# Reordering the partitions of a recurrent stage, summing the step size in PSUM, and moving one C product to GpSimd

## The reference, cut to what matters

```python
h = layer_norm(x)                              # x: 8 sequences x 256 x 128
u, z = split(h @ in_w)                         # 256 channels each
u = silu(conv(u))                              # 4 taps
dbl = u @ xw                                   # 64 + 16 + 16 columns: rank, B, C
dt = softplus(dbl[:64] @ dtw + dtb)            # step size, 256 channels
h_t = exp(dt_t * A) * h_(t-1) + (dt_t * u_t) * B_t     # 16 states for each channel
y_t = sum over states of h_t * C_t,  + u * D
x = x + (y * silu(z)) @ ow
```

## Time and profile before

| | |
|---|---|
| median of three runs | 1708.91 us (1708.18 to 1709.97) |
| the profiled execution | 1705.7 us |
| its span, first to last instruction | 1704.0 us |
| recurrent stage in it | scans from 499.97 to about 1315.9 us |
| busy in the whole span | PE 1337.6, DVE 1387.7, ACT 1311.6, POOL 1075.3 us |
| mean granted TensorE clock | 0.924 of 2.4 GHz |

### The profile page before, as it was taken

The page is one execution under the profiler, slowest core; times in us unless marked ns, Lnnn a source line. Parts: engine busy times, 40 slices in busy tenths (PEclk is TensorE's granted clock), DMA queues, the critical chain, the costliest instruction groups (busy, mean ns, idle before and its releaser), DMA issues. The chain is left out here.

```text
span 1704.0 us, 25209 instructions
## 1 busy us (share of the span) xinstructions
PE 1337.6 (78%) x7544; PEld 694.5 (41%) x7547; DVE 1387.7 (81%) x2394; ACT 1311.6 (77%) x2978; POOL 1075.3 (63%) x714
## 2 busy tenths in 40 slices
PE   6777898996677776867776877767756899899989
PEld 4554555553322222332222332222322466566543
DVE  4655788896529999999999999999998588778835
ACT  4444787884658999999999999999975788777730
POOL 2001566661048999999999999999996254444410
PEclk9999899997978889999989988999977999999979
DMA  3000000001045434455434545443440511121000
GB/s 105 2 1 2 1 2 2 1 2 26 7 174 208 178 122 173 164 210 199 165 132 165 200 167 199 174 146 147 185 150 25 185 51 51 51 99 50 1 1 25
DMA packets 70229, 168.19 MB, mean 99 GB/s; under 512 B 20420, under 2 KB 40152, under 8 KB 56664
## 3 DMA queue, kind: packets, MB, share of 16 engines
q1 hardware_dynamic: 68680, 166.17, 27.1%
q10 hardware_dynamic: 1168, 0.53, 0.1%
q0 software_dynamic: 256, 0.01, 0.0%
HBM read 131.04 MB, written 35.65 MB: 98 GB/s over the span
## 5 line engine op out<-in xcount | busy, mean ns | idle before, releaser
L1785 POOL TENSOR_TENSOR ma_hs<-ma_dtuR,ma_Bt 128x1024 f32<-128x1024 f32 x192 | 449.4, 2369 | 12.3 <-DMA ma_dtuR<-ma_dtu_d 6.9
L914 POOL TENSOR_TENSOR x_pr<-x_pr,x_rec 128x512 f32<-128x512 f32 x256 | 267.9, 1047 | 244.2 <-DVE x_rec L1203 244.2
L1162 ACT ACTIVATE x_pr<-x_sm,x_mx 128x256 f32<-128x256 f32 x512 | 255.4, 500 | 62.6 <-DVE x_mx L1194 58.8
L1868 PE MATMUL ps<-ma_hs,ma_fold 128*32 128x512 f32 x1024 | 157.7, 744 | 180.4 <-DVE ma_hs L2204 172.3
L2016 ACT ACTIVATE ps<-ma_dtR,ma_A 128x512 f32<-128x512 f32 x384 | 248.7, 680 | 48.6 <-DVE ma_hs L2204 41.4
L1793 POOL TENSOR_TENSOR ma_hs<-ma_hs,ma_Ct 128x1024 f32<-128x1024 f32 x112 | 264.2, 2370 | 22.3 <-DVE ma_hs L2198 21.9
L2198 DVE TENSOR_TENSOR_SCAN ps<-ps,ma_hs 128x1024 f32<-128x1024 f32 x112 | 255.9, 2285 | 7.9 <-ACT ps L2016 7.9
L2046 ACT ACTIVATE ma_rowB<-ma_dtuT,ma_BT 128x128 f32<-128x128 f32 x512 | 232.8, 525 | 1.3
L2198 DVE TENSOR_TENSOR_SCAN ma_hs<-ps,ma_hs 128x1024 f32<-128x1024 f32 x80 | 180.7, 2275 | 5.3 <-ACT ps L2016 5.3
L2204 DVE TENSOR_TENSOR ma_hs<-ps,ma_Ct 128x1024 f32<-128x1024 f32 x144 | 176.3, 1224 | 5.0
L990 PE MATMUL ps<-ident,x_pr 128*128 128x128 f32 x1024 | 154.2, 283 | 17.1 <-ACT x_pT L1076 12.7
(11 more groups left out here) (325 smaller groups left out, 2594.7 us busy)
## 6 DMA issues: line engine op xcount, KB each, us to landing
ma_dtuR<-ma_dtu_d SPq DMA_DIRECT2D x32, 1024.0 KB, 6.8
ma_dtR<-ma_dt_d SPq DMA_DIRECT2D x32, 1024.0 KB, 6.6
ma_Bt<-ma_bc_d SPq DMA_DIRECT2D x16, 1024.0 KB, 5.0
ma_Ct<-ma_bc_d SPq DMA_DIRECT2D x16, 1024.0 KB, 7.4
ma_dtu_d<-ma_dtu SPq DMA_DIRECT2D x32, 256.0 KB, 2.0
ma_dt_d<-ma_dt SPq DMA_DIRECT2D x32, 256.0 KB, 2.3
keys_d<-ma_kv SPq DMA_DIRECT2D x32, 256.0 KB, 2.6
values_d<-ma_kv SPq DMA_DIRECT2D x32, 256.0 KB, 2.0
```

Of the source, the lines that this page charges most:

```text
L914: pool.tensor_tensor(pr[:, r, :, :], pr[:, r, :, :], rec[:, r, :].unsqueeze(2).broadcast_to([P, 2, L]), ALU.mult).then_inc(pr_done, 1)
L1162: a = act.activation(pr[:, n % RP, t, :], sm[:, n % 2, t, :], ACT.Exp, bias=mx[:, n % 2, t:t + 1], scale=-1.0, accum_out=den[:, n % RP, t: ...
L1785: pool.tensor_tensor(hs[:, k % SLOTS, :, :], dtuR[:, h, q, :].unsqueeze(1).broadcast_to([P, 2, CH]), rows(Bt, k), ALU.mult).then_inc(dbu_d ...
L1868: mm = pe.matmul(c.ps[q * E32:(q + 1) * E32, Y[h], :], fold[:, :], hs[:, (k0 + q) % SLOTS, a, :], start=False, stop=(j % 2 == 1 and a == 1 ...
```

## The change

It has three parts. (1) The partitions are ordered p = 32n + e, so that `scale_rows` reads and writes runs without gaps; the strided step goes to `copy_dtu`, which reads PSUM with a step of four elements. `fold`, the loads of A and the broadcasts of B, C, dt and dtu follow the new order. (2) The step size is summed in PSUM: softplus(v) = v/2 + |v/2| + ln(1 + exp(-2|v/2|)). The weights are halved once a block (`half_steps`), TensorE adds |v/2| and later the logarithm to the banks PA and PB through the identity (`add_to_dt`, four matmuls a round), ACT copies the sum to `dt` without the first columns, and DVE computes dt x u straight from PSUM. POOL's product and its memsets go; the first columns are set once. (3) `NORM_D` becomes 1, 2, 3, 6, 7, 8, 13 and 15: eight C products on DVE and eight on POOL.

```diff
-                             g["m_al"][i].rearrange("(h e q) (n o) -> h q e n o", h=2, q=gq, o=4)[h, q]).then_inc(done, 16)
+                             g["m_al"][i].rearrange("(h e q) (n o) -> h q n e o", h=2, q=gq, o=4)[h, q]).then_inc(done, 16)
...
-    NORM_D = set(range(16)) - {0, 5, 9, 10, 11, 12, 13}
+    NORM_D = set(range(16)) - {0, 4, 5, 9, 10, 11, 12, 14}
...
-        rowB = s.sb("rowB", [P, 4, 2, GQ, E32, NI])
+        rowB = s.sb("rowB", [P, 4, 2, GQ, NI, E32])
...
                     for h in range(2):
                         sp.wait_ge(dtu_done, 2 * F + h + 1)
                         sp.dma_start(dtu_d[d, h], dtu[:, h, :]).then_inc(dt_out[h], 16)
+                        sp.wait_ge(dt_done, 2 * F + 2 - h)
                         sp.dma_start(dt_d[d, h], dt[:, h, :]).then_inc(dt_out[h], 16)
                     def spread(dst, src, h, done):
                         sp.dma_start(dst[:, h, :, :].rearrange("p q t -> p (q t)"),
-                                     src[d, h].rearrange("(e a q) t -> e a (q t)", a=1, q=GQ)
-                                     .broadcast_to([E32, NI, GQ * CH])).then_inc(done, 16)
+                                     src[d, h].rearrange("(a e q) t -> a e (q t)", a=1, q=GQ)
+                                     .broadcast_to([NI, E32, GQ * CH])).then_inc(done, 16)
...
+                for h in range(2):
+                    pool.memset(by_seq(dt[:, h, :])[:, :, 0:1], BIG).then_inc(consts, 1)
...
-                def dt_times_u(F):
-                    for h in range(2):
-                        pool.wait_ge(dt_done, 2 * F + h + 1)
-                        pool.tensor_tensor(dtu[:, h, :], dt[:, h, :], u[:, F % 2, h, :], ALU.mult).then_inc(first_set, 1)
-                        pool.wait_ge(first_set, 2 * F + h + 1)
-                        pool.memset(by_seq(dt[:, h, :])[:, :, 0:1], BIG).then_inc(dtu_done, 1)
...
                 def dt_projection(F):
                     b = (F // QUARTERS) % 2
+                    pe.wait_ge(half_dt, F // QUARTERS + 1)
...
-                        pe.matmul(c.ps[:, bank, :], w_dt[:, b, h * P:(h + 1) * P], xp[:, :], start=True, stop=True
-                                  ).then_inc(dt_ps, 1)
+                        pe.matmul(c.ps[:, bank, :], w_dt[:, b, h * P:(h + 1) * P], xp[:, :], start=True, stop=False,
+                                  skip_group_check=True).then_inc(dt_ps, 1)
+
+                def add_to_dt(F, ready, added, stop):
+                    pe.wait_ge(ready, F + 1)
+                    for h, bank in ((0, PA), (1, PB)):
+                        mm = pe.matmul(c.ps[:, bank, :], c.ident[:, :], dtu[:, h, :], start=False, stop=stop,
+                                       skip_group_check=True)
+                    mm.then_inc(added, 1)
...
                     if 0 <= f < NF:
                         pe.wait_ge(kv_done, 4 * f + 1)
                         kv_job(4 * f + 1, Y[1])
+                    if F < NF:
+                        add_to_dt(F, abs_done, abs_added, False)
+                        add_to_dt(F, ln_done, ln_added, True)
+                    if 0 <= f < NF:
                         sum_y(f, 1)
...
                     if F < NF:
                         pe.wait_ge(dt_done, 2 * F + 2)
+                        pe.wait_ge(dtu_done, 2 * F + 2)
                         turn_b(F)
...
-                    act.activation(dtuT[:, :, :].rearrange("p t e -> p (t e)"), c.ps[:, PB, :], ACT.Copy).then_inc(dtuT_done, 1)
+                    act.activation(dtuT[:, :, :].rearrange("p t (q e) -> p t q e", q=GQ),
+                                   c.ps[:, PB, :].rearrange("p (t e q) -> p t q e", t=4, q=GQ), ACT.Copy).then_inc(dtuT_done, 1)
...
-                    act.activation(rowB[:, t, a, :, :, ni], dtuT[:, t, :].rearrange("p (e q) -> p q e", q=GQ), ACT.Copy,
+                    act.activation(rowB[:, t, a, :, ni, :], dtuT[:, t, :].rearrange("p (q e) -> p q e", q=GQ), ACT.Copy,
                                    scale=BT[:, f % 2, t, a, ni:ni + 1]).then_inc(rows_done, 1)
...
                 def exponential(F):
-                    act.wait_ge(abs_done, F + 1)
-                    act.activation(dtu[:, :, :], dtu[:, :, :], ACT.Exp, scale=-1.0).then_inc(exp_done, 1)
+                    act.wait_ge(abs_added, F + 1)
+                    act.activation(dtu[:, :, :], dtu[:, :, :], ACT.Exp, scale=-2.0).then_inc(exp_done, 1)
...
+                def step_size(F):
+                    act.wait_ge(ln_added, F + 1)
+                    if F >= 1:
+                        act.wait_ge(dt_out0, 32 * F)
+                        act.wait_ge(dt_out1, 32 * F)
+                    for h, bank in ((1, PB), (0, PA)):
+                        if h == 0:
+                            act.wait_ge(dtu_done, 2 * F + 1)
+                        act.activation(by_seq(dt[:, h, :])[:, :, 1:L], by_seq(c.ps[:, bank, :])[:, :, 1:L],
+                                       ACT.Copy).then_inc(dt_done, 1)
+
+                def half_steps(i):
+                    act.wait_ge(weights_in, LOADS * (i + 1))
+                    act.wait_ge(consts, 2)
+                    act.activation(w_dt[:, i % 2, :], w_dt[:, i % 2, :], ACT.Copy, scale=0.5).then_inc(half_dt, 1)
...
+                            if t == 8:
+                                step_size(F)
...
-                def step_size(F):
-                    if F >= 1:
-                        dve.wait_ge(dt_out0, 32 * F)
-                        dve.wait_ge(dt_out1, 32 * F)
-                    dve.wait_ge(ln_done, F + 1)
+                def dt_times_u(F):
+                    dve.wait_ge(ln_added, F + 1)
                     for h, bank in ((0, PA), (1, PB)):
-                        dve.scalar_tensor_tensor(out=dt[:, h, :], in0=c.ps[:, bank, :], scalar=0.0, in1=dtu[:, h, :],
-                                                 op0=ALU.max, op1=ALU.add).then_inc(dt_done, 1)
+                        if h == 1:
+                            dve.wait_ge(dt_done, 2 * F + 1)
+                        dve.tensor_tensor(dtu[:, h, :], c.ps[:, bank, :], u[:, F % 2, h, :], ALU.mult).then_inc(dtu_done, 1)
...
                         if t == 8 and F < NF:
-                            step_size(F)
+                            dt_times_u(F)
```

More of the change, by code:

```diff
@@ L1725, in _ @@
                         sp.dma_start(dst[:, d, :, :].rearrange("p o t -> p (o t)"),
-                                     bc_d[d, k * NS:(k + 1) * NS, :].rearrange("(a n o) t -> a n (o t)", a=1, o=NO)
-                                     .broadcast_to([E32, NI, NO * CH])).then_inc(done, 16)
+                                     bc_d[d, k * NS:(k + 1) * NS, :].rearrange("(n a o) t -> n a (o t)", a=1, o=NO)
+                                     .broadcast_to([NI, E32, NO * CH])).then_inc(done, 16)
                     if f >= 0:
@@ L1730, in _ @@
                         kv_store(sp, 4 * f + 1)
+                    if F == 0:
+                        sp.wait_ge(consts, 5 + NI)
                     for h in range(2):
@@ L1760, in _ @@
             def _(pool):
-                pool.memset(fold[:, :], 1.0).then_inc(consts, 1)
+                pool.memset(fold[:, :], 0.0).then_inc(consts, 1)
                 pool.wait_ge(consts, 1)
@@ L1765, in _ @@
                 pool.memset(xp[XB:XB + 1, :], 1.0).then_inc(consts, 1)
[L1766 to L1770, removed]
-                                   base=NI - 1, pattern=[[NI, E32]], channel_multiplier=-1).then_inc(consts, 1)
+                for ni in range(NI):
+                    pool.wait_ge(consts, 3 + ni)
+                    pool.affine_select(out=fold[:, :], in_=fold[:, :], compare_op=ALU.not_equal, fill=1.0,
+                                       base=-E32 * ni, pattern=[[-1, E32]], channel_multiplier=1).then_inc(consts, 1)
+                for h in range(2):
+                    pool.memset(by_seq(dt[:, h, :])[:, :, 0:1], BIG).then_inc(consts, 1)
                 def rates(i):
@@ L1813, in _ @@
                             times_c(k)
-                        if t == 8 and f + 1 < NF:
-                            dt_times_u(f + 1)
                         if f % QUARTERS == 1 and i < NBLK:
@@ L1924, in turn_rows @@
                             mm = pe.transpose(c.ps[:, 2 * (k % 2) + a, t * P:(t + 1) * P],
-                                              rowB[:, t, a, q, :, :].rearrange("p e n -> p (e n)"), c.ident[:, :])
+                                              rowB[:, t, a, q, :, :].rearrange("p n e -> p (n e)"), c.ident[:, :])
                     mm.then_inc(turned, 1)
@@ L1929, in _ @@
                 average(0)
-                pe.wait_ge(consts, 5)
+                pe.wait_ge(consts, 3 + NI)
                 for f in range(-1, NF + 1):
@@ L2110, in _ @@
                 rates(0)
+                half_steps(0)
                 affine(0)
@@ L2116, in _ @@
                 logarithm(0)
+                step_size(0)
                 copy_b(0)
@@ L2167, in _ @@
```

(3 more changed lines are left out.)

5 lines of the change are left out of this document (2 added, 3 removed).

## The result

The changed kernel takes 2218.05 us (median; 2214.53 to 2220.14), the kernel before 1709.44 (1708.18 to 1710.71) on the same chip: ratio 1.297, 95% interval 1.295 to 1.300. It is 509 us slower, where 1699.4 was forecast. The profiled execution has a span of 2217.3 us.

What follows compares the result with a forecast made beforehand. DVE was taken as the nearest bound, with ACT and PE arriving nearly together at scan 12; rounds 8.4 and last two 5.0 less start 3.9 gave -9.5 us, so 1699.4 us in the runs, range 1686 to 1720.

Steps and rivals of the forecast that it cites:

- Without cost: the loads and broadcasts in the new order (same sizes, 8 KB or 16 bytes a run as before): Loads and broadcasts in the new partition order, counted at nothing because sizes and run lengths stay the same.
- the four rivals: DVE stays the bound, 1688 us; PE takes all back, 1708; copies no faster, 1727; clock falls before the first addition, 1736.
- Rounds: In 14 rounds scan 12 starts 0.6 us earlier each (0 to 1.4), 8.4 us together.
- Last two rounds: Item 13's product hides in scan 14's stall for PE; the two products taken off DVE count, 2 x 2.5 = 5.0 us.
- The start: Ahead of the first round nothing hides the additions and copies; dt's first store and the first scan come 3.9 us later.
- The second addition at half clock: PE's addition after the logarithm, idle 4.4 us before, runs at 1.2 GHz in many rounds: 3.7 to 4.1 us, not 2.0.
- Scan 12 waits for PE, at +24.5: Counted from scan 4, PE's work ahead of `turn_rows` 12 comes last; scan 12 starts at +24.5 instead of +25.06.
- rival 1: DVE stays the bound: PE keeps 2.4 GHz, scan 12 starts at +23.65, each round gains 1.4, time 1688; chance 0.24.
- Rival 3, the copies: Scaled copies save under about 0.06 us each, so ACT is late at scan 12: +18 us, time 1727; chance 0.10.
- Eight products: 20.3 us at most in the rounds: Eight instead of nine C products on DVE: 16 rounds x 1.27 us, the most the change can bring there.
- `copy_dtu` without surcharge: Its stride of four on the PSUM side counted at zero; the dear end was 0.6 us, at item 15.

Runs made afterwards that it cites:

- experiment 2: The changed kernel with each of the six large broadcast reads issued as four DMAs to 32 partitions, 32 rows outermost: 1699.35 us, ratio 0.995.
- experiment 12: The changed kernel in the old partition order, whole reads 32 outermost, only the scaled copies' input side made contiguous: 1695.72 us, ratio 0.994.
- experiments 5 and 11: On the kernel before: 5 only the eight C products, 1698.15 us; 11 those plus the scaled copies' input side made contiguous, 1700.62 us.
- Experiment 6: The kernel before with the step size summed in PSUM and the eight products, old partition order, strided copies and whole reads: 1722.65 us, ratio 1.008.
- experiment 3: The changed kernel with only the reads of dt and dt x u cut into four, B and C left at 4 outermost: 1882.27 us, ratio 1.102.

## Why the prediction was wrong, step by step

**The step that failed: "Without cost: the loads and broadcasts in the new order (same sizes, 8 KB or 16 bytes a run as before)".** I compared bytes, run lengths and the number of DMAs, found them equal, and stopped. The order of the pattern's dimensions, which the diff shows, I did not price. Measured: 0 forecast, 519 us at the changed kernel (2218.05 less 1699.35), 512 on the kernel before. None of the four rivals contained it, so the range left it out as well. The trace of before held the warning in part: bursts of 350 GB/s say that the round's reads use nearly all engines and are hidden only because of that.
The Trainium skill has the rule, in "DMA: Bandwidth & Descriptors" (Why a DMA increments its semaphore by 16 and not by 1): the number of engines is the largest one up to 16 that divides the slowest dimension of both patterns. On the same page the Trainium skill's "Rules for kernel authors" add that a leading broadcast of c copies confines a DMA to c engines at most. The traces agree: 0.24 of 16 engines and four packets at once at 4 outermost, eight at once at 8, sixteen at 16. I had weighed the copies against the skill, and not the reads.

With this step mended (experiment 2: 1699.35 us) the forecast of 1699.4 is met, but that is in good part luck: the start costs 8 us more than forecast, and the stage and the later stages give 3 us more each. By its terms:

- *Rounds*, forecast 14 x 0.6 = 8.4 us: from scan 4 of the first round to scan 4 of the fifteenth experiment 2 takes 701.7 us, the kernel before 710.5, so 8.7 or 0.62 a round. The number is right and the place is not. I had all of it in the stretch from scan 4 to scan 12 and had said that the stretch from scan 12 to the next scan 4 keeps its length. The first shrank by 0.17 us on average (24.58 to 24.41), the second by 0.44 (26.16 to 25.72). The round that I read, with scan 12 at +25.06, was the latest of the sixteen; the median is +24.40, already ahead of the +24.5 that I forecast for the new kernel. What shortened the other stretch stays open.
- *Last two rounds*, forecast 5.0: they give 7.1. Scan 14 waited 2.96 and 3.00 us for PE in them before and starts without a wait in experiment 2 (at 1258.83 and 1305.35), where I had expected about 3 us again. The rest of the 16.6 us by which the stage is shorter, 0.8, lies in the first items. In experiment 12 the stage is 15.1 us shorter.
- *The start*, forecast 3.9: the first scan is 11.8 us later in experiment 2, where ACT waits 7.0 us for the cut reads, and 8.1 in experiment 12. Less the jitter of 3.4 seen in experiments 5 and 11, 12's 4.7 us agree with the forecast; the rest belongs to the cut reads. What is left of experiment 2's gain, some 3 us, lies in later stages.
- *The second addition at half clock.* PE in experiment 2, the additions, `sum_y(f,1)` and `turn_rows` 12:
```profile
683.70 1.98 PE L1856 MATMUL ps<-ma_dtu,ident 128*128 128x512 f32 x4 [0.82 <-ACT ma_dtu L2100]
689.97 3.52 PE L1856 MATMUL ps<-ma_dtu,ident 128*128 128x512 f32 x4 [4.29 <-ACT ma_dtu L2109]
693.42 1.92 PE L1870 MATMUL ps<-ma_hs,ma_fold 128*32 128x512 f32 x16
...
701.09 1.04 PE L1926 MATMUL ps<-ident,ma_rowB 128*128 128x128 f32 x8
```
  3.7 to 4.1 us after 4.4 us of idleness was forecast, 3.52 after 4.29 measured, in a window (690 to 694) whose mean granted clock is 0.61. But `sum_y` behind it takes 1.92 us (granted clock 1.00 from 693.4 to 695.3), where it took 3.64 after a gap of 8.15: the addition pays the slow start, and what follows runs at full clock. I had 2.1 us lost in all; it is about 1.5 (3.52 less 1.98).
- *Scan 12 waits for PE, at +24.5.* DVE in the same round, scan of item 4, dt x u and scan 12:
```profile
678.47 4.47 DVE L2225 TENSOR_TENSOR_SCAN ma_hs<-ps,ma_hs 128x1024 f32<-128x1024 f32 x2 [0.34 <-ACT ps L2023]
...
693.53 1.32 DVE L2210 TENSOR_TENSOR ma_dtu<-ps,ma_u 128x512 f32<-128x512 f32 x2 [0.21 <-PE ps L1856]
...
702.17 2.29 DVE L2225 TENSOR_TENSOR_SCAN ma_hs<-ma_hs,ps 128x1024 f32<-128x1024 f32 x1 [0.16 <-PE ps L1926]
```
  It starts at +23.7 (702.17 less 678.47), after a wait of 0.16 for PE. In this round that is rival 1's number (+23.65). But most rounds are of three kinds, at +23.6 to +23.7, +24.5 and +25.0, with a median of +24.5; so the forecast's position is met, while rival 1's gain of 1.4 us a round is not: it is 0.62.
- *Rival 3, the copies.* Its price was +18 us and its point a saving of 0.06 us a copy. Experiment 6 is that rival made (no saving): +14 us. With 84 ns saved (experiment 12) the loss is gone in full. The size holds roughly; the point lies between 0 and 84 ns, and no run stands nearer to 60.
- *Eight products: 20.3 us at most in the rounds.* Beside parts 1 and 2 they bring 21.5 us (1720.9 to 1699.4), of which 17.1 in the stage, so the bound holds; alone they bring 10.5. And *part 2* costs 24.5 us on top of part 3 with slow copies and brings 12.5 with fast ones (1711.9 to 1699.4). The parts can't be priced singly and added; the timeline of a round, with all three in it, was the right place to work.
- *`copy_dtu` without surcharge*: 574 ns a copy against 575, with a step of four on the PSUM side. The doubt that the prediction drew from the Trainium skill ("SBUF — State Buffer", Door 1: The DMA port swizzle) is not borne out here; what that page says of strided PSUM access, it says of matmuls, and this is a copy on ScalarE.

## What to carry to other kernels

When a layout changes, write down each DMA's pattern before and after and read the outermost dimension first; with 4 or 8 there, as in these runs, multiply its time by 16 over that number, and ask when the data is wanted, since a burst wanted within 10 us is not hidden by a round of 51. If the new order forces a small outermost dimension, cut the transfer into several (519 us back here), or get the benefit from the side of the layout that no DMA sees: sorting one on-chip copy gave two thirds of the copies' saving without touching a DMA. And test one edit at a time: one line of this change gave 10 us, as much as the best kernel with all the rest, and two expressions cost 512. Last, when a sum hangs on one place in a round, read that place in every round: the one read here was the latest of sixteen.

## What the runs showed of the hardware

- Equal bytes in small pieces aren't equal work. Cut into four DMAs to 32 partitions, the reads' 8 KB packets take 606 ns (median, 500 to 1316 us) instead of 309. Windows of the stage in experiment 2:
```profile
500.00:1316.00 816.00, 654.40 (x2540) 260.69 (x2540) 771.78 (x461) 704.63 (x1394) 760.23 (x338) 0.92 0.69 167
```
  and of experiment 12, whose reads are as before:
```profile
500.00:1316.00 816.00, 655.32 (x2546) 259.56 (x2544) 772.35 (x461) 712.89 (x1394) 760.95 (x338) 0.92 0.45 167
```
  At the same 167 GB/s the share is 0.69 and 0.45. Why, these runs don't settle.
- A confined read also delays transfers that are issued behind it and are not confined themselves: stores of dt landed after 17.1 us instead of 2.3 in the kernel after, and after 15.9 instead of 2.5 in experiment 3, where only B and C are confined.
- In ScalarE's copies with a step of four elements (128 x 128) the step costs 129 ns of throughput, 84 of it on the side read.
